# Side work of an attention pipeline put into other slots, its first group projected through four PSUM banks, and squares on ScalarE

## The reference

```python
x = x + L0_xattn(layernorm(x), ctx, Wq, Wk, Wv, Wo, q_norm_w, k_norm_w, pos, draft_pos)
x = x + L0_ffn(layernorm(x), ...)        # 32 experts, top 6
x = x + L1_xattn(layernorm(x), ctx, ...) # each token sees 9 context rows
x = x + L1_ffn(layernorm(x), ...)

# L0_xattn, 16 heads of 128 over 4 key heads:
kv_in = concat([ctx, tokens], axis=1)                 # 1857 rows
q, k, v = tokens @ Wq.T, kv_in @ Wk.T, kv_in @ Wv.T
q, k = rope(rms_norm(q) * q_norm_w), rope(rms_norm(k) * k_norm_w)
out = softmax(q @ k.T / sqrt(128)) @ v @ Wo.T
```

## Time and profile before

| | us |
|---|---|
| median of three runs (1933.8 to 1937.72) | 1936.93 |
| the profiled execution | 1938.12 |
| its span, first to last instruction | 1936.3 |
| TensorE busy | 1715.0 (89%) |
| VectorE busy | 1424.1 (74%) |
| GpSimd busy | 1102.6 (57%) |
| ScalarE busy | 1091.3 (56%) |

### The profile page before, as it was taken

The page is one execution under the profiler, slowest core; times in us unless marked ns, Lnnn a source line. Parts: engine busy times, 40 slices in busy tenths (PEclk is TensorE's granted clock), DMA queues, the critical chain, the costliest instruction groups (busy, mean ns, idle before and its releaser), DMA issues. The chain is left out here.

```text
span 1936.3 us, 41490 instructions
## 1 busy us (share of the span) xinstructions
PE 1715.0 (89%) x14548; PEld 1308.0 (68%) x14679; DVE 1424.1 (74%) x3798; ACT 1091.3 (56%) x2728; POOL 1102.6 (57%) x1718
## 2 busy tenths in 40 slices
PE   3789899998999998989999999976999999079997
PEld 2567677787777777877777877754555555038974
DVE  6787887878967878878788788755756775675746
ACT  3567676766676766667666666652133332073543
POOL 3586676865957767768568577410256664072210
PEclk9999999999999999999999999996999999595998
DMA  3112101010100110001001000325379995510100
GB/s 120 56 45 72 37 24 62 18 40 22 49 23 18 34 42 18 26 21 36 19 18 35 24 2 23 107 76 208 123 220 270 272 269 178 160 32 16 45 10 27
DMA packets 74650, 140.24 MB, mean 72 GB/s; under 512 B 10922, under 2 KB 44819, under 8 KB 74195
## 3 DMA queue, kind: packets, MB, share of 16 engines
q1 hardware_dynamic: 63634, 105.37, 17.9%
q0 software_dynamic: 9984, 30.42, 4.6%
q10 hardware_dynamic: 832, 1.84, 0.3%
HBM read 111.73 MB, written 25.86 MB: 71 GB/s over the span
## 5 line engine op out<-in xcount | busy, mean ns | idle before, releaser
L887 DVE TENSOR_TENSOR att_pT<-att_pT 128x512 bf16<-128x512 f32 (+1 forms) x512 | 319.5, 650 | 196.0 <-ACT att_pT L702 194.4
L549 PE MATMUL att_out<-att_V,att_pT 128*128 128x128 bf16 x5760 | 387.2, 219 | 27.3 <-DVE att_pT L887 20.3
L549 PEld LDWEIGHTS att_out<-att_V,att_pT 128*128 128x128 bf16 x5760 | 348.9, 98 | 59.0 <-DVE att_pT L887 25.5
L702 ACT ACTIVATE att_pT<-att_pT 128x512 bf16<-128x512 f32 (+1 forms) x512 | 277.0, 569 | 176.6 <-PE att_pT L535 176.6
L708 ACT ACTIVATE att_prob<-att_scores,att_negmax 128x512 f32<-128x512 f32 (+1 forms) x512 | 329.7, 653 | 31.9 <-DVE att_negmax L876 31.9
L526 PE MATMUL att_scores<-att_K,att_Q 128*128 128x512 bf16 (+1 forms) x1408 | 296.1, 359 | 8.0 <-DVE att_K L849 1.4
L874 DVE TENSOR_REDUCE att_mx<-att_scores 128x1 f32<-128x512 f32 (+1 forms) x512 | 291.3, 630 | 0.6 <-PE att_scores L526 0.6
L535 PE MATMUL att_pT<-att_ident,att_prob 128*128 128x128 f32 x1920 | 274.2, 274 | 0.0
L526 PEld LDWEIGHTS att_scores<-att_K,att_Q 128*128 128x128 bf16 x1536 | 150.6, 98 | 145.0 <-issue 2.2
L449 PE MATMUL att_aux<-att_wkv,att_kvT 128*128 128x256 bf16 x1440 | 187.9, 282 | 34.2 <-DVE att_aT L849 16.8
L535 PEld LDWEIGHTS att_pT<-att_ident,att_prob 128*128 128x128 f32 x1920 | 208.6, 141 | 0.8
(11 more groups left out here) (332 smaller groups left out, 3144.6 us busy)
## 6 DMA issues: line engine op xcount, KB each, us to landing
moe_wa<-in_wa_l SPq DMA_DIRECT2D x80, 480.0 KB
att_wq<-wq_s SPq DMA_DIRECT2D x12, 512.0 KB, 3.6
att_wo<-wo_s SPq DMA_DIRECT2D x12, 512.0 KB, 3.8
moe_y<-y_s SPq DMA_DIRECT2D x8, 768.0 KB, 4.6
att_stage<-in_ctx_l SPq DMA_DIRECT2D x9, 512.0 KB, 4.0
near_s<-att_windows POOLq DMA_DIRECT2D x8, 576.0 KB, 5.4
win_near<-near_s SPq DMA_DIRECT2D x32, 144.0 KB
moe_wb<-in_wb_l SPq DMA_DIRECT2D x80, 48.0 KB
```

Source lines behind the costliest of these rows:

```text
L549: last = nc.tensor.matmul(out_ps[:, i % 2, :], pT[:, i % 2, a, k, :], V[:, par, k, w, :], start=(k, a, w) == (0, 0, 0), stop=(k, a) == (KT ...
L702: nc.scalar.activation(pT[:, i % 2, 0, 4 * j:4 * j + m, :], pT_ps[j % 2][:, 0:m, :], ACT.Copy).then_inc(s["pt_hi"], 1)
L887: nc.vector.tensor_tensor(pT[:, i % 2, 1, 4 * j:4 * j + m, :], pT_ps[j % 2][:, 0:m, :], pT[:, i % 2, 0, 4 * j:4 * j + m, :], ALU.subtract) ...
```

## The change

In group 0 the tokens are turned ahead of every projection, and the projections go in turn through the four score banks, not through `aux`; a bank is waited for only when its row set of four projections ago has been copied. The turned keys wait until all rows have been copied out of these banks. The sums of squares of group 0 go from VectorE to ScalarE (`squares`). Ropes of other row sets go to GpSimd, and VectorE takes the low halves of two turned tiles ahead of its last rope.

In all groups the side work is moved. On TensorE and ScalarE it now stands inside the slot, after the scores and after the copies of the first two turned quarters; on VectorE it stays at the slot's end, and the low half of a split is taken in its own slot, not one later. The rows of the second attention are made in slot 3, not 7, the mean row in slot 2 of a batch's last group, the tokens of the next batch are turned in slot 0 of its third group, not slot 4, and the absolute values and the sines are parted (slots 1 and 7 of the third group). Splits and angle steps get other slots by tables (a row or two of each is shown).

```diff
-FIRST_GROUP = [("KV", 1), ("XT", 0), ("KV", 0), ("KV", 2), ("Q", 0), ("KV", 3), ("KV", 4), ("Q", 1), ("KV", 5), ("KV", 6),
-               ("KV", 7), ("QT", 0), ("QT", 1), ("KT", 0), ("KT", 1), ("KT", 2), ("KT", 3)]
-FIRST_ON_POOL = [("KV", 0), ("KV", 3), ("KV", 5)]
+FIRST_GROUP = [("XT", 0), ("KV", 1), ("KV", 2), ("KV", 0), ("Q", 0), ("KV", 3), ("KV", 4), ("KV", 5), ("Q", 1), ("KV", 6),
+               ("KV", 7), ("KT", 0), ("QT", 0), ("KT", 1), ("QT", 1), ("KT", 2), ("KT", 3)]
+FIRST_ON_POOL = [("KV", 2), ("KV", 3), ("KV", 6)]
+FIRST_LOWS = [("KV", 7), ("KT", 0), ("QT", 0)]
...
-JOBS_AT = [((0, 0), ("wo", 0)), ((0, 2), ("wkv", 2)), ((0, 3), ("wq", 2)), ((0, 5), ("ctx", 1, 0)), ((0, 6), ("wo", 1)),
...
+JOBS_AT = [((0, 0), ("wo", 0)), ((0, 2), ("wkv", 2)), ((0, 6), ("wq", 2)), ((0, 7), ("wo", 1)),
...
 for _b in range(2, B):
-    JOBS_AT += [((4 * _b - 4, 1), ("ctx", _b, 0)), ((4 * _b - 4, 5), ("ctx", _b, 1)), ((4 * _b - 3, 1), ("ctx", _b, 2)), ((4 * _b - 3, 5), ("ctx", _b, 3))]
+    JOBS_AT += [((4 * _b - 3, 2), ("ctx", _b, 0)), ((4 * _b - 3, 6), ("ctx", _b, 1)), ((4 * _b - 2, 2), ("ctx", _b, 2)), ((4 * _b - 2, 6), ("ctx", _b, 3))]
...
+TRIG_AT = {(0, 3): (0,), (0, 7): (1, 2), (1, 0): (3,), (1, 3): (4,), (1, 7): (5,), (2, 0): (6,)}
+ABS_AT, SINES_AT = (2, 1), (2, 7)
+STATS_AT, NORMALISE_AT, TURN_AT = (0, 0), (1, 0), (2, 0)
+NEAR_SLOT, SUMS_AT, MEAN_AT = 3, (3, 0), (3, 2)
...
+            if g == 0 and kind in ("KV", "Q"):
+                k = FIRST_ROWS.index((kind, n)) % NB
+                return scores[:, 512 * k:512 * k + 512]
...
-                    if gt or kind not in ("KT", "QT"):
+                    if gt or kind in ("AT", "WO"):
                         aux_free(s[FREE[kind]], nth(kind, n, gt))
+                    elif kind in ("KV", "Q"):
+                        k = FIRST_ROWS.index((kind, n)) - NB
+                        if k >= 0:
+                            pe.wait_ge(s[FREE[FIRST_ROWS[k][0]]], nth(*FIRST_ROWS[k], 0))
+                    elif kind == "KT":
+                        pe.wait_ge(s["kvraw_ready"], PAIRS)
+                        pe.wait_ge(s["qraw_ready"], 2)
                     if kind == "KV":
                         context_ready(gt, n)
...
                     if not last:
                         form_scores(g, u, i)
+                        b, at = g // KVH, (g % KVH, i)
+                        if at == TURN_AT and b + 1 < B:
+                            turn_tokens(b + 1)
+                        if at == MEAN_AT:
+                            mean_row(b)
+                        if i == NEAR_SLOT:
+                            near_keys(g)
...
-                    if (g % KVH, i) == (2, 4) and b + 1 < B:
-                        turn_tokens(b + 1)
-                    if (g % KVH, i) == (3, 7):
-                        mean_row(b)
-                    if i == 7:
-                        near_keys(g)
...
+                def squares(kind, n):
+
+                    if kind == "KV":
+                        act.wait_ge(s["kvraw_ready"], nth(kind, n, 0))
+                        for q in range(pair(n)):
+                            last = nc.scalar.activation(kp[:, 2 * n + q, :], kvraw[:, n % 4, q, 0:HD], ACT.Square, scale=float(HD) ** -0.5, accum_out=kss[:, n % 4, q:q + 1])
+                        last.then_inc(s["k_ss"], 1)
+                    elif kind == "Q":
+                        act.wait_ge(s["qraw_ready"], nth(kind, n, 0))
+                        for q in range(REP):
+                            last = nc.scalar.activation(qp[:, n, q, :], qraw[:, n, q, :], ACT.Square, accum_out=qss[:, n, q:q + 1])
+                        last.then_inc(s["q_ss"], 1)
 
...
+                        if (g, i) in SPLIT_AT:
+                            split_high(SPLIT_AT[g, i])
+                        if at == ABS_AT and b + 1 < B:
+                            absolute(b + 1)
+                        if at == SINES_AT and b + 1 < B:
+                            sines(b + 1)
+                        if at == TURN_AT and b + 1 < B:
+                            tokens_high(b + 1)
+                        if at == MEAN_AT:
+                            mean_row(b)
+                        if i == NEAR_SLOT:
+                            near_raw(g)
...
+                for j in range(3):
+                    start_high(j)
+                tokens_high(0)
+                for j in range(3, 6):
+                    start_high(j)
+                absolute(0)
                 sines(0)
-                start_high(3)
-                start_high(4)
-                after = {("XT", 0): [5], ("KV", 6): [6], ("KV", 7): [7]}
+                after = {("KV", 6): 6, ("KV", 7): 7}
                 for kind, n in FIRST_GROUP:
                     if kind == "XT":
-                        tokens_high(0)
-                    else:
-                        task(kind, n, 0, 0, 0)
-                        values_high(kind, n, 0, 0)
-                    for j in after.get((kind, n), ()):
-                        start_high(j)
+                        continue
+                    task(kind, n, 0, 0, 0)
+                    squares(kind, n)
+                    values_high(kind, n, 0, 0)
...
-                    late = (g, i - 1) if i else (g - 1, TILES - 1)
-                    if late in SPLIT_AT:
-                        split_low(SPLIT_AT[late])
-                    if (r, i) == (2, 4) and b + 1 < B:
-                        tokens_low(b + 1)
+                    b, at = g // KVH, (g % KVH, i)
                     if b + 1 < B:
-                        if r == 1 and i < TRIG_STEPS:
-                            trig_step(b + 1, i)
-                        if (r, i) == (0, 4):
+                        if at == STATS_AT:
                             token_stats(b + 1)
-                        if (r, i) == (1, 7):
+                        if at == NORMALISE_AT:
                             normalise(b + 1)
-                    if (r, i) == (3, 0):
+                        if at == TURN_AT:
+                            tokens_low(b + 1)
+                        for k in TRIG_AT.get(at, ()):
+                            trig_step(b + 1, k)
+                    if (g, i) in SPLIT_AT:
+                        split_low(SPLIT_AT[g, i])
+                    if at == SUMS_AT:
...
+                for j in range(2):
+                    start_low(j)
+                tokens_low(0)
+                for j in range(2, 5):
...
+                order = [it for it in FIRST_GROUP if it[0] in ("KV", "Q") and it not in FIRST_LOWS] + FIRST_LOWS[1:] + FIRST_LOWS[:1]
+                order += [it for it in FIRST_GROUP if it[0] in ("KT", "QT") and it not in FIRST_LOWS]
+                for kind, n in order:
                     task(kind, n, 0, 0, 0)
                     raw_rows(kind, n, 0, 0)
```

61 lines of the change are left out of this document (20 added, 41 removed).

## The result

The changed kernel takes 1884.45 us (median of 4 runs, 1882.4 to 1885.26) against 1937.33 of the kernel before: a ratio of 0.9729, interval 0.9713 to 0.9746. The forecast was 1885. The profiled execution spans 1881.9 us, 54.4 less than before.

| part | how it is read | forecast | measured |
|---|---|---|---|
| A, ahead of slot 0 | first scores 70.04, now 57.13 | -13 | -12.9 |
| B, the slots | from there to the last addition to x: 1231.0, now 1204.7 | -27 | -26.3 |
| C, the end | from that addition to the next block: 13.0, now 1.4 | -11.8 | -11.6 |
| the rest of the program | 622.2, now 618.7 | 0 | -3.6 |

The account below looks back on a forecast made before the run. Groups without side work were taken as bound by TensorE; side work adds TensorE waiting. Savings of 13, 27 and 11.8 us sum to 51.8, from 1938.12 to 1886.3; the median 1.2 lower, 1885 us, range 1870 to 1902.

Parts of the forecast that it names:

- Part A: Ahead of slot 0 of the first group: first scores start at 56.6 us, 13 us earlier; bounds 6 and 17.
- TensorE does not decide here: Ahead of slot 0: TensorE's ten projections, 2.72 us each from 17.93, end near 45, before the first scores at 56.6.
- at its lower level of 1.2 GHz: Ahead of slot 0: the clock assumed for TensorE's ten projections, 2.72 us each, ending near 45 us.
- list lies below GpSimd's: Ahead of slot 0: VectorE's work was taken to be shorter than GpSimd's, with 3 us to lose if not.
- The port: Rival ahead of slot 0: VectorE and GpSimd take turns throughout, leaving a gain of 6 us: 1892 us, chance 0.12.
- Part B: The attention's slots: moved side work, priced by engines' idle time in its new place, saves 27 us; bounds 13 and 38.
- two new waits: Third groups: token halves in slot 0 add 2.5 us, sines in slot 7 add 2.1; group 6 takes 78.9.
- Only moved: Rival on the slots: VectorE's idle times shrink, half the gain comes back elsewhere, 27 becomes 13: 1899 us, chance 0.13.
- The bank: Near rows in slot 3, not 7: TensorE's 0.37 us wait for the bank goes, -0.4 us a group.
- Part C: End of the attention block: GpSimd's gathers end before the last addition to x, saving 11.8 us; bounds 9 and 13.
- Four slots earlier: Last group: near rows made in slot 3 let GpSimd's 23 us of stores and gathers end well before 1301 us.
- The slower rival: Slot 3: ScalarE's copy of near rows waits for the earlier rows' store, losing 60 us: 1945 us, chance 0.03.

## Why the prediction was right

That the median came out within 0.6 us is partly luck. The sum missed the profiled execution by 2.6 us (1886.3 for 1883.7), most of it the 3.6 of the rest, and the median, which was taken 1.2 below that execution, lies 0.75 above it.

**Part A.** The size held, -12.9 for -13, and half of its reasons did not. "TensorE does not decide here" holds for the changed kernel, but only because of the four banks: with one bank it decides, at a price of 5.0 us. That it stays "at its lower level of 1.2 GHz" was wrong: the projections end at 35.0, not 45. That VectorE's "list lies below GpSimd's" was wrong too: from 24.77 on VectorE waited 0.95 and 0.47 us for norms and worked for the rest, and its list decides, as the squares (+4.4) and the ropes (-1.3) show. The sum came out by luck in part: the length of a rope was read from a row that already held its meetings with VectorE, and both lists end within 1.3 us of each other.

**The port.** Its mechanism is there, its price was not. VectorE's operations from 24.8 us to the first scores take 34.6 us, 8.6 more than at each one's shortest, and giving it three more ropes made it quicker. But part A did not shrink to 6 us, as that rival had it, since the prices already contained the meetings.
The Trainium skill ("SBUF — State Buffer", section "SBUF: two separate sides") has the shared pair as an exclusive lock held for a whole instruction, against VectorE operations with two SBUF inputs where GpSimd's operation reads SBUF too. The trace of the kernel with all ropes on VectorE agrees: 1.24 and 2.20 us beside halves of 1.43 and 2.16, 0.28 alone.

**Part B.** -26.3 for -27. Groups 4 and 5 came out at 73.84 and 75.11 (forecast 74.3 and 75.3), group 6 at 78.81 (78.9), its two new waits within 0.2 us. Group 2 was mis-sized: 81.76 for 79.8, and 10: 80.03 for 78.9. What the forecast left out is that TensorE's waiting was followed by stretches at 1.2 GHz: in slot 0 of group 2 its busy time fell from 11.40 to 9.70 when the wait was taken away, and slot 7, behind the sines, takes 11.03 and 11.15 us in groups 2 and 10 for 9.94 in group 6. The other groups were some tenths better and paid for it. "Only moved" falls: the groups have lost TensorE's idle time for good. But I priced the steps by the slots' idle times alone, and the undone place inside the slot shows that this was half of the story: 17.9 us come back where ScalarE's splits and sines stand at the slot's end, ahead of the next slot's copies. The bank, by which the near rows were priced, is the small part of it, 0.1 to 0.4 a group.
The Trainium skill's 2.66 us for a change of tables ("ScalarE: Activation LUTs", section "What ACT_TABLE_LOAD costs") would, by an estimate (78.9 and twice 1.38), have made group 6 some 81.7. The measured 78.81 goes with the load of 1.28 alone, and with the steps at the slot's end the load starts 0.02 us behind the activation before it (599.90) and the sine 0.02 behind the load.

**Part C.** -11.6 for -11.8, and GpSimd's 22 to 23 us from rows to barrier as read. "Four slots earlier" was only half of what did it: with slot 7 kept, the wait at the end was still 6.4 shorter than the 13.0 of before, 4.1 of it by the place inside the slot. The slower rival, a copy waiting for a store in slot 3, did not come: in the view of waits (engine, line, releaser, us, times, longest) the copy waits 16 times, once in a group, each time for its product.

```profile
ACT att_raw L791 <- PE att_aux L522: 34.6, 16, 2.4
```

**The rest**, 3.6 us that no term had. Ahead of the next block all but GpSimd had stood idle for 13 us in the kernel before, and the clock stood at 1.2 GHz from 1305.2 to 1339.4; in the changed one it did so from 1266.0 to 1272.7 and again from 1276.1 to 1286.3. So the router's first products, counted from the start of that block, were done 1.9 us sooner. With the end late the rest took 622.2 and 621.9; with the end early 615.1 to 621.2 in twelve kernels. The direction fits an effect of the idle end; how much of the 3.6 it is stays open, since kernels with the same end differ by more, and the mean clock of the whole rest is 0.88 in both.

## What to carry to other kernels

Price a moved step twice: by the idle time of its in-order engine in that slot, and by what is queued behind it on that engine at that point of the slot; here each half undone alone took back most of the gain. A wait seen in the trace is not yet its price: the 0.69 us for the bank came back as 0.1 to 0.4 a group. Before sharing elementwise work between VectorE and GpSimd, sum up what VectorE's operations take beside GpSimd's and what the same ones take alone: if the difference is as long as the work that is given away, keep it. A wait of TensorE can cost twice, once as a wait and once as a stretch at half clock behind it.
